# Splitting the second chunk one slot earlier, signalling its spread image by image, and reordering ScalarE in odd slots

## What is computed

```python
h = relu6(bn(conv(x, ternarize(w1)), ...))             # L0: 1x1, 32 -> 192
h = relu6(bn(conv(h, ternarize(w2), padding=1), ...))  #     3x3, 192 -> 192
x = x + bn(conv(h, ternarize(w3)), ...)                #     1x1, 192 -> 32
...
x = relu(bn(conv3x3(quant(relu(bn(conv3x3(quant(x), quant(w)))))), ...) + x)   # L1: 8 bit
x = relu(bn(conv3x3(x, w) + b))                        # L2, channels with a tiny maximum set to 0
x = relu(bn(conv3x3(x, w) + b))                        # L3, the same
```

## Time and profile before

| | us |
|---|---|
| median of 3 runs | 267.81 |
| lowest and highest of them | 267.43, 267.94 |
| the profiled execution's own time | 268.13 |
| its span on the core | 266.3 |
| PE busy in the span | 234.2 |
| DVE busy | 233.2 |
| ACT busy | 184.2 |

### The profile page before, as it was taken

The page is one execution under the profiler, slowest core; times in us unless marked ns, Lnnn a source line. Parts: engine busy times, 40 slices in busy tenths (PEclk is TensorE's granted clock), DMA queues, the critical chain, the costliest instruction groups (busy, mean ns, idle before and its releaser), DMA issues.

```text
span 266.3 us, 5565 instructions
## 1 busy us (share of the span) xinstructions
PE 234.2 (88%) x2151; PEld 133.3 (50%) x2151; DVE 233.2 (88%) x466; ACT 184.2 (69%) x274; POOL 8.7 (3%) x26
## 2 busy tenths in 40 slices
PE   0659999099999989999998999999997999789982
PEld 0315555056555445655454555555643555446651
DVE  3799989927999899999989999889878948999994
ACT  5799896348666467866458757969342747997962
POOL 4400000000000000000000000000000000000003
PEclk9999999859999999999999999999999999999997
DMA  7327100200002100001200000000000000254306
GB/s 238 99 62 241 40 1 15 75 2 0 2 0 70 25 0 2 1 2 32 60 2 0 4 0 0 2 2 1 0 2 1 2 0 0 55 118 103 88 19 241
DMA packets 7098, 10.72 MB, mean 40 GB/s; under 512 B 2176, under 2 KB 5216, under 8 KB 7072
## 3 DMA queue, kind: packets, MB, share of 16 engines
q1 hardware_dynamic: 6880, 10.33, 14.1%
q10 hardware_dynamic: 192, 0.04, 0.1%
HBM read 4.04 MB, written 1.61 MB: 21 GB/s over the span
## 4 chain that ended last, share of the span: by engine, by line
DVE 37%; PE 34%; issue 11%; ACT 8%; DMA 5%; SPq 3%; DVEq 0%; ACTq 0%
PE ps L533 10%; PE ps L522 5%; PE ps L708 4%; PE ps L544 4%; DVE hs L1251 3%; DVE h2a L1299 3%; PE ps L555 3%; DVE ps L1278 3%; DVE hs L1243 2%; DMA big<-w2b_in 2%; PE ps L643 2%; DVE h2a L1294 2%; DVE big L1587 1%; DVE cmx L1632 1%; DMA xk<-xpart 1%
## 5 line engine op out<-in xcount | busy, mean ns | idle before, releaser
L533 PE MATMUL ps<-vv,w2at 128*128 128x378 f16 (+1 forms) x192 | 38.2, 336 | 0.6 <-DVE ps L1278 0.6
L828 ACT ACTIVATE ra<-ps,bn 128x392 f32<-128x392 f32 x32 | 21.4, 675 | 19.9 <-PE ps L479 19.2
L522 PE MATMUL ps<-vv,wu 128*128 128x392 f16 x180 | 34.8, 329 | 0.0
L746 PE MATMUL ps<-big,wst 128*32 128x378 f16 (+10 forms) x576 | 24.5, 326 | 3.6 <-DVE big L1587 2.2
L533 PEld LDWEIGHTS ps<-vv,w2at 128*128 128x128 f16 x192 | 17.9, 99 | 15.8 <-issue 5.1
L708 PE MATMUL ps<-qi,wqi 128*128 128x378 bf16 (+7 forms) x144 | 23.9, 325 | 0.6 <-ACT qi L1027 0.6
L522 PEld LDWEIGHTS ps<-vv,wu 128*128 128x128 f16 x180 | 17.4, 98 | 12.1 <-DVE vv L1261 0.2
L860 ACT ACTIVATE hs<-ug,magic 128x784 f16<-128x784 f16 x16 | 15.2, 948 | 11.1 <-DVE ug L1232 11.1
L874 ACT ACTIVATE r2a<-ps,bn 128x784 f32<-128x784 f32 x15 | 15.1, 1003 | 10.7 <-DVE h2a L1299 10.7
L746 PEld LDWEIGHTS ps<-big,wst 128*32 128x32 f16 x576 | 15.2, 96 | 13.0 <-issue 2.2
L533 PE MATMUL ps<-vv,w2bt 128*128 128x378 f16 (+1 forms) x96 | 21.2, 330 | 0.0
(11 more groups left out here) (218 smaller groups left out, 443.6 us busy)
## 6 DMA issues: line engine op xcount, KB each, us to landing
xk<-xpart SPq DMA_DIRECT2D x45, 49.0 KB, 1.9
xin<-x_in SPq DMA_DIRECT2D x4, 392.0 KB, 3.8
big<-part SPq DMA_DIRECT2D x25, 49.0 KB, 2.0
big<-big SPq DMA_DIRECT2D x3, 392.0 KB, 3.6
y_out<-xin SPq DMA_DIRECT2D x3, 392.0 KB, 2.4
big<-w2a_in SPq DMA_DIRECT2D x3, 288.0 KB, 4.3
big<-w2b_in SPq DMA_DIRECT2D x6, 144.0 KB, 4.0
y_out<-xin SPq DMA_DIRECT2D x2, 196.0 KB, 2.4
```

The source lines that it names most:

```text
L522: i = nc.tensor.matmul(landing(slice(0, P), PBANK[k], dx), weights(raw, mid, k, dx, False), moving(s, k, dx, b), start=(n == 0 and dx == D ...
L533: i = nc.tensor.matmul(landing(slice(0, P), PBANK[k], dx), weights(raw, mid, k, dx, False), moving(s, k, dx, b), start=False, stop=(n == 2 ...
L746: i = nc.tensor.matmul(img(ps[C * g:C * g + C, bank + h, :W * n], n)[:, to[0], to[1]], wst[:, layer, C * t:C * t + C], kst[:, KBUF[layer][ ...
L828: nc.scalar.activation(ra[:, 0, HALF * h:HALF * h + HALF], ps[:, bank, :HALF], ACT.Relu, bias=bn[:, BSH, BN1A:BN1A + 1], scale=bn[:, BSC, ...
```

## The change

Three things change, all of them in order and signalling; every instruction of before is there after, with the same shapes.

1. The split of chunk 1 moves up: on DVE `split_second(1)` stands right behind `split_first(1)` in slot (0, 0); on ACT `x_high(1, 0)` stands ahead of the first `relu_rest` of slot (0, 0) and `x_high(1, 1)` behind `relu_a` there.
2. The spread has a third semaphore, `s_second`: an image's three DMAs signal `s_first` (g = 0), `s_second` (g = 1) or `s_xk` (g = 2 and 3). `expand_rest(j)` waits for the first two if j % 4 is 0, and for `s_xk` if j % 4 is 2; `expand_main` waits only for image 2.
3. In ACT's slots g = 1, `relu_b(j-1)` and `copy_y(j)` now stand ahead of `relu_main(j+2, 0)`; slots g = 3 keep their order. In the odd slots `relu_rest(j+3, 0)` now stands ahead of `add_shift`.

```diff
@@ SP, spread
+                    landed = s_first[c] if g == 0 else s_second[c] if g == 1 else s_xk[c]
                     for k in range(3):
                         sp.dma_start(xk[C * k:C * k + C, G * c + g, :],
-                                     xpart[C * g:C * g + C, c % 2, k, :]).then_inc(s_first[c] if g == (0 if c else 1) else s_xk[c], 16)
+                                     xpart[C * g:C * g + C, c % 2, k, :]).then_inc(landed, 16)
@@ PE, expand_main
-                    if j >= G and j % G == 0:
-                        pe.wait_ge(s_first[j // G], 48)
-                    if j == 2 or j >= G and j % G == 1:
-                        pe.wait_ge(s_xk[j // G], XK[j // G])
                     if j == 2:
+                        pe.wait_ge(s_xk[0], XK)
                         pe.wait_ge(rb_ready, 4)
@@ PE, expand_rest
-                    if j >= G and j % G == 0:
+                    if j % G == 0:
                         pe.wait_ge(s_first[j // G], 48)
-                        pe.wait_ge(s_xk[j // G], XK[j // G])
+                        pe.wait_ge(s_second[j // G], 48)
+                    else:
+                        pe.wait_ge(s_xk[j // G], XK)
@@ ACT, slot
-                    if ahead and not even:
+                    if ahead and g == G - 1:
                         relu_main(j + 2, 0)
                     relu_b(j - 1)
                     copy_y(j)
-                    if ahead and even:
+                    if ahead and g < G - 1:
                         relu_main(j + 2, 0)
                 if ahead:
                     relu_main(j + 2, 1)
                 if begin:
+                    x_high(1, 0)
                     relu_rest(j + 2, 0)
...
                 relu_a(j)
-                if not begin:
+                if begin:
+                    x_high(1, 1)
+                else:
                     copy_m1(j + 1)
...
+                if not even and j + 3 < B:
+                    relu_rest(j + 3, 0)
                 if g == 1:
                     add_shift(c)
-                if not even and j + 3 < B:
-                    relu_rest(j + 3, 0)
@@ DVE, slot
                 if begin:
                     split_first(1)
+                    split_second(1)
```

More of the change, by code:

```diff
@@ L85 @@
 V_DUP = [(0, 0), (1, 0), (1, 1), (1, 2), (1, 3)]
-XK = [16 * 3 * (G - 2)] + [16 * 3 * (G - 1)] * (NCH - 1)
+XK = 16 * 3 * (G - 2)
 TOTAL_BANK = {1: 4, 2: 4, 3: 7, 4: 7, 5: 7, 6: 7}
@@ L209, in conv_seq @@
         s_first = [sem(f"s_first{c}") for c in range(NCH)]
+        s_second = [sem(f"s_second{c}") for c in range(NCH)]
         s_xk = [sem(f"s_xk{c}") for c in range(NCH)]
@@ L258, in wait, with spread_landed @@
                 eng.wait_ge(s, n)
+        def spread_landed(eng, c):
+            if c:
+                eng.wait_ge(s_first[c], 48)
+            eng.wait_ge(s_second[c], 48)
+            eng.wait_ge(s_xk[c], XK)
         def stack_free(eng, layer, c):
@@ L456, in expand_one @@
                 if n == 0:
-                    pe.wait_ge(s_first[0], 48)
+                    pe.wait_ge(s_second[0], 48)
                 nc.tensor.matmul(ps[:, bank, :HALF], (w1t[:, 0:P], w1t[:, P:P + 2 * HB])[two],
@@ L786, in x_high @@
                 if c >= 2:
-                    act.wait_ge(s_first[c - 2], 48)
-                    act.wait_ge(s_xk[c - 2], XK[c - 2])
+                    spread_landed(act, c - 2)
                 act.wait_ge(*((s_x[c], 16) if k == 0 else (xr_ready, c + 1)))
@@ L996, in _ @@
             slot(0, 0, first=True)
-            x_high(1, 0)
-            slot(0, 1, first=True, split=(1, 1))
+            slot(0, 1, first=True)
             slot(0, 2, first=True, split=(2, 0))
@@ L1159, in split_second @@
                 if c >= 2:
-                    dve.wait_ge(s_first[c - 2], 48)
-                    dve.wait_ge(s_xk[c - 2], XK[c - 2])
+                    spread_landed(dve, c - 2)
                 tt(xpart[:, c % 2, 2, :], xrest[:], high(xrest[:]), ALU.subtract).then_inc(x_split, 1)
@@ L1434, in _ @@
             slot(0, 0, first=True)
-            split_second(1)
             slot(0, 1, first=True)
```

## The result

| | before | after |
|---|---|---|
| median, us | 267.88 (4 runs) | 258.77 (4 runs) |
| lowest and highest | 267.43, 268.01 | 258.00, 260.03 |
| profiled execution | 268.13 | 258.00 |
| its span | 266.3 | 256.2 |

After to before the ratio is 0.9667, with a 95% interval of 0.9623 to 0.9712. The forecast was 257.7 with a range of 256.8 to 260.4. For the profiled execution the sum said 258.0, and it took 258.00. Part of such scatter is found further down, ahead of the first slot. The two slowest runs here (259.28 and 260.03) have no trace, so what slowed them stays open.

What follows compares the result with a forecast made beforehand. DVE was taken to lead after 62 us, PE half a step behind. Gains of 7.80 + 0.86 + 0.86 + 0.59 = 10.1 us took the profiled 268.13 to 258.0, so the median to 257.7 (range 256.8 to 260.4).

Steps and rivals of the forecast that it cites:

- the sum: Whole kernel: DVE gains of 7.80 + 0.86 + 0.86 + 0.59 = 10.1 us, taken from the profiled 268.13.
- DVE leads after 62 us, PE follows: L0 after 62 us: DVE sets the pace; PE, gaining 9.2 us, follows DVE's 7.80 with 1.4 in hand.
- The first chunk, 7.80: DVE's first chunk: 0.69 from the earlier split, 5.34 and 1.77 from waits at `seed_pair(2)` and `grid_main(4)`.
- The hole goes without the new signalling: PE's 6.42 us idle before `expand_rest(4, 0)`: the earlier split closes it; the new semaphore is worth 0 to 0.2 us.
- ACT's order, 0.86 + 0.86 + 0.59: Slots (1, 1), (2, 1), (3, 1): DVE's waits for `cy` go, worth 0.86, 0.86 and 0.59 us.
- `relu_rest` ahead of `add_shift`: Slots (1, 1), (2, 1): saves PE 1.10 us each, DVE nothing directly; without it PE becomes the bound by (2, 1).
- The slower rival: Slots g = 1: PE waits 1.6 us and the clock falls, 4 x 4.4 = 17.6 us lost, 277.5; chance 0.02.
- The median: Whole kernel: median forecast at 257.7 us, as the profiled execution before stood 0.32 above its runs' median.
- The 258.0 for the profiled execution: Whole kernel: the profiled 268.13 us less 10.1 us gives 258.0 for the profiled execution after.

Runs made afterwards that it cites:

- e1: The kernel before with only the split of chunk 1 moved up, old signalling and old ACT order: median 260.59 us, against 268.13 before.
- e4: The changed kernel, but PE waits for all twelve spread DMAs of chunk 1 as before: median 258.30 us.
- e6: The changed kernel with `relu_b` and `copy_y` again behind the first `relu_main` in slots g = 1: median 260.84 us.
- e2: The kernel before with only ACT's new order in odd slots: median 265.62 us, against 268.13 before.
- e7: The changed kernel with `add_shift` again ahead of `relu_rest` in slots g = 1: median 258.30 us.
- e5: The changed kernel run once more, nothing altered: median 258.08 us over five runs.
- e3: The kernel before with only the spread signalled image by image, so PE waits for six DMAs, not twelve: median 263.96 us.
- e8: The changed kernel with the four split subtractions of chunks 2 and 3 moved from DVE to GpSimd: 260.46 us.

## Why the prediction was right, point by point

- *DVE leads after 62 us, PE follows.* Shown by e1 (7.5, not 9.2) and by the waits of before that come back unchanged. In the trace after, DVE has no wait over 0.2 us from 33 to 157 us.
- *The first chunk, 7.80.* Right: `seed_pair(2)` comes 20.81 us behind `seed_pair(0)` after (53.11 - 32.30) and 26.81 before (59.21 - 32.40), 6.00 against 0.69 + 5.34 = 6.03; the next slot is shorter by 1.79 (12.06 to 10.27), against 1.77. e1 measured 7.53, with the 0.23 of its early wait lost.
- *The hole goes without the new signalling.* Right: behind `seed_pair(1)` e4 loses nothing. Here the size was a little off: SP's issues cost 0.68 us each in e4 (8.13 / 12) and 0.71 after (8.52 / 12), where I had 0.62, so the twelve DMAs were 0.37 us late for PE in e4 and 0.90 in e1. PE had that much in hand.
- *ACT's order, 0.86 + 0.86 + 0.59.* e6 loses 2.21, e2 gains 2.19 apart from the clock (3.13 - 0.94). At the seeds of the trace after the first two steps are 0.87 each, and the last is 0.47 (10.01 - 9.54) where 0.59 was forecast.
- *`relu_rest` ahead of `add_shift`.* This step failed. I wrote that without it PE would eat 0.86 of each wait out of what it has in hand and become the bound by slot (2, 1). e7 shows no PE wait over 0.2 us at `expand_rest` in slots (1, 1) and (2, 1), and L0 behind `seed_pair(1)` is not longer (149.88 us). The wait of 0.93 in the earlier trace rows had two sides. ACT's half keeps its place relative to DVE: the first `relu_rest` of slot (1, 1) starts 5.80 us behind `seed_pair(5)` in the trace of before (99.16 - 93.36) and in e7 (90.59 - 84.79). PE's does not: its first `expand_rest` comes 3.77 us behind that seed before (97.13 - 93.36) and 4.63 in e7 (89.42 - 84.79), 0.86 later, because PE is held at `expand_main(7, 0)` by DVE's `residual`, ahead of DVE's gain (82.97, 0.25 <-DVE). So with `cy` early the wait is nearly gone without the swap. The prediction had kept that wait at its old length.
- *The slower rival* (pauses on PE at every odd slot, and a falling clock) did not come: the granted clock is 1.00 in the stretches between 30 and 196 us, with waits of up to 0.89 us in them.
- *The median.* I carried the 0.32 us between profile and median over from before. After, the first set's median lies 0.77 above its profiled execution and e5's 0.18. That step has no ground: part of the difference depends on the block ahead of L0, whose length changes from run to run.
- *The 258.0 for the profiled execution.* That it came out to the hundredth is luck. L0 gave 10.01 of the 10.11 us, and 0.10 came from ahead of it (32.40 to 32.30), which the change does not touch.

## What to carry to other kernels

When two engines are equally busy, look which of them has the unbroken run of work behind a hole: the gain is that engine's own wait, not the size of the hole on the other one. A wait between two engines that a change moves by different amounts should be worked out anew from both sides before a cure for it is counted. Starting a transfer earlier can make a finer signal for it nearly worthless; each of the two alone looked large here (7.5 and 4.2 us). And where two kernels differ by a few tenths, look in their traces at which point the difference arises: here 0.22 and 0.23 us looked like the worth of two edits and arose ahead of both.

## What the runs showed of the hardware

- PE's granted clock fell to its lower level in the hole of 6.42 us (0.98 between 50 and 52 us, 0.50 in the next two) and just behind one of 2.68 us (e3, 0.58 between 50 and 52). Behind shorter waits it stayed at 1.00: 0.90 in e1, 1.10 in e8 (at 72.91) and 1.47 in the trace after (at 221.48).
- The same 18 products ahead of L0, in kernels that are equal up to there, took from 4.13 to 5.65 us, by how many of them ran at the low clock. It moved the first seed by up to 0.86 us and another wait by 0.23, more than the parts e4 and e7 are worth.
- A GpSimd subtraction over 784 columns took 1.49 to 2.26 us where DVE needs 0.97, and held up DVE instructions beside it by 0.42 to 1.29 us each, a `tensor_scalar` of 0.36 us most of all. Two DVE instructions with an input in PSUM kept their 1.04 us beside it.
